# First FFN of a four-stage layer: two batches as dense expert pairs, two as tiles of chosen rows, with their QKV and key choice beside the attention

## The reference

```python
x = x + attn_a(layernorm(x))   # Haar wavelet mixing: q and v, transform over tokens, product, inverse, W_out
x = x + ffn(layernorm(x))      # 8 experts 128 -> 256 -> 128, relu squared; top 2 of softmax(x Wg), weights renormalised
x = x + attn_b(layernorm(x))   # 16 heads of 8; three softmaxes: band |i-j|<=128, top 128 keys of each head by score, first 64 keys
x = x + ffn(layernorm(x))
```

## Time and profile before

| what | us |
|---|---|
| median of 3 runs | 567.24 (566.62 to 568.09) |
| profiled execution | 567.43 |
| span of its instructions | 565.6 |
| PE busy | 517.7 (92%) |
| DVE busy | 405.7 (72%) |
| ACT busy | 349.4 (62%) |
| POOL busy | 271.4 (48%) |

### The profile page before, as it was taken

How to read it: one execution, slowest core, us unless ns; L and a number is a source line. 1 busy time by engine, 2 the same in 40 slices (tenths; PEclk the granted TensorE clock), 3 DMA queues, 4 the chain that set the end, 5 groups by cost and what they waited for, 6 DMA issues and landing times.

```text
span 565.6 us, 13219 instructions
## 1 busy us (share of the span) xinstructions
PE 517.7 (92%) x4483; PEld 320.4 (57%) x4483; DVE 405.7 (72%) x1426; ACT 349.4 (62%) x775; POOL 271.4 (48%) x429
## 2 busy tenths in 40 slices
PE   5899999999996889988998899999998999889996
PEld 2477776767672545444544454555545553567875
DVE  2547575698999799999967878788788795135335
ACT  6476666666640266666775577666775667667753
POOL 2402030160605994675408985859917246264540
PEclk9999999999996899999999999999999999999999
DMA  7970000000000000000000000001100011574606
GB/s 230 348 263 2 1 1 1 0 2 1 11 2 13 2 16 13 9 9 16 12 14 5 15 12 9 9 20 30 34 9 9 18 41 43 200 264 164 207 21 187
DMA packets 33443, 31.99 MB, mean 57 GB/s; under 512 B 7250, under 2 KB 28502, under 8 KB 33376
## 3 DMA queue, kind: packets, MB, share of 16 engines
q1 hardware_dynamic: 31616, 27.80, 15.9%
q0 software_dynamic: 1760, 3.35, 1.7%
HBM read 8.57 MB, written 12.00 MB: 36 GB/s over the span
## 4 chain that ended last, share of the span: by engine, by line
PE 62%; DVE 23%; issue 7%; POOL 3%; ACT 3%; DMA 1%; SPq 0%; DVEq 0%; POOLq 0%; ACTq 0%
PE BANK L1568 6%; PE BANK L1550 6%; PE BANK L1673 5%; PE BANK L1618 5%; PE BANK L1648 4%; PE BANK L1676 3%; DVE SW L1178 3%; PE BANK L1679 2%; PE BANK L1504 2%; PE BANK L1514 2%; DVE X L1160 2%; DVE M L1176 2%; PE BANK L1643 2%; PE BANK L1623 2%; POOL OH L556 2%
## 5 line engine op out<-in xcount | busy, mean ns | idle before, releaser
L822 ACT ACTIVATE PT<-BANK 128x256 f32<-128x256 f32 (+2 forms) x352 | 158.5, 492 | 96.6 <-PE BANK L1648 75.5
L556 POOL TENSOR_SCALAR OH<-IOTA,POS 128x128 bf16<-128x128 bf16 x240 | 139.5, 601 | 1.4 <-DVE POS L1192 1.0
L1219 DVE CUSTOM_DVE_ANT_0 XN_a<-BANK,BANDQ 128x256 f32<-128x256 f32 (+1 forms) x128 | 62.3, 487 | 23.2 <-PE BANK L1618 19.6
L1568 PEld LDWEIGHTS BANK<-W,PT 128*128 128x128 f32 x512 | 62.0, 192 | 15.2 <-issue 14.3
L1219 DVE CUSTOM_DVE_ANT_0 XN_c<-BANK,BANDQ 128x384 f32<-128x384 f32 (+1 forms) x128 | 62.3, 487 | 10.7 <-PE BANK L1618 9.6
L1568 PE MATMUL BANK<-W,PT 128*128 128x128 f32 x512 | 62.5, 275 | 0.0
L1550 PE MATMUL BANK<-XNT_ALL,W 128*128 128x512 f32 x128 | 60.6, 597 | 0.0
L733 ACT ACTIVATE PT<-BANK 128x512 f32<-128x512 f32 x64 | 38.0, 597 | 31.5 <-PE BANK L1550 31.0
L563 POOL TENSOR_TENSOR SUM<-NRM 128x128 f32<-128x128 f32 x16 | 7.3, 455 | 102.7 <-DVE NRM L1240 102.7
L1673 PE MATMUL BANK<-PT,V 128*32 128x256 f32 (+1 forms) x512 | 47.7, 444 | 2.0 <-ACT OS L831 0.4
L1224 DVE TENSOR_REDUCE QST<-BANK 128x4 f16<-128x512 f32 x64 | 41.6, 688 | 7.6 <-PE BANK L1623 7.5
(11 more groups left out here) (312 smaller groups left out, 1201.8 us busy)
## 6 DMA issues: line engine op xcount, KB each, us to landing
xs<-W SPq DMA_DIRECT2D x1, 6984.0 KB, 25.1
KZB<-W SPq DMA_DIRECT2D x16, 256.0 KB, 2.4
KZC<-W SPq DMA_DIRECT2D x15, 256.0 KB, 2.6
...
```

Source lines behind the costliest of these rows:

```text
L556: last = nc.gpsimd.tensor_scalar(OH[g % 2][:, i, t, :], IOTA[:, :], POS[:, t, c:c + 1], None, ALU.is_equal)
L822: nc.scalar.activation(PT[u % PT_RING][:, 0:w], P2_BANK[u % SCORE_RING][:, 0:w], ACT.Exp, scale=SCALE).then_inc(S["exp_done"], 1)
L1219: nc.vector.tensor_tensor_reduce(out=JUNK[v % 2][:, 0:n], in0=P1_BANK[v % SCORE_RING][:, 0:n], in1=BANDQ[:, off:off + n], scale=1.0, scala ...
L1568: last = mm(DOWN_BANK[n % 2][:, t * P:(t + 1) * P], HID_T[n % 2][hh][:, t * P:(t + 1) * P], W2[:, e, hh, :], start=(hh == 0), stop=(hh == ...
```

## The change

1. **Head.** Batches 0 and 1 run as two interleaved chains with buffers and banks of their own (CHAIN, CHAIN_BANK). ACT scales q by band while it copies it, and DVE multiplies it with v straight from PSUM. x of batch 1 is loaded second. `keep_busy` shrinks from 46 to 17 matmuls and uses zeros of W12. `with_bias` for batches 0 and 1 waits until both are normalized. The a steps of batches 2 and 3 go beside the pairs, 3 pairs apart.
2. **First FFN.** Only batches 0 and 1 are dense: 16 pairs. Batches 2 and 3 are routed as in the second FFN (class `Wave`, EARLY beside LATE): route at pairs 7 and 10, 16 scatters on POOL, table at pairs 11 and 12, then 23 tiles with their own row buffer and two result banks (`D_BANK["early"]`) instead of one. SP fills two DRAM areas with zeros instead of one. The results are loaded in four transfers, and POOL (not DVE) adds them to X.
3. **QKV of batches 0 and 1.** Batch 0 beside pairs 8 to 14. Batch 1 beside tiles 2 to 5.
4. **Key choice of batches 0 and 1.** Scores at tile 3, one or two half rounds a tile from tile 4, the last four behind the tiles, then mask, marks, places and the one-hots of group 0 between the first maxima. The spread of group 0's keys is issued at tile 11, and the gather of group 1 moves into group 0 at unit 2.
5. **Batches 2 and 3.** Statistics, normalization, transposes, scores and QKV move into groups 0 to 4 (C_AT, STATS_C, NORMS_C), through MISC. Their rounds move from groups 0 to 4 to groups 1 to 4.
6. **Batch 1's stacks and values** are split between ACT and POOL in groups 0 and 1, as those of batches 2 and 3 were already.

The core of the diff:

```diff
-SCORES_AT = (2, 3)
...
-MORE_ROUNDS = {(g, u) for g in range(5) for u in range(1, 22, 3)} - {(4, 13), (4, 16), (4, 19)}
-A_PERIOD = 5
...
+MORE_ROUNDS = {(g, u) for g in range(1, 5) for u in (1, 4, 6, 9, 12, 15, 17, 20)}
+A_PERIOD = 3
...
+EARLY = Wave("early", 2, 2)
+LATE = Wave("late", 0, 3)
+PAIRS = EARLY.first * E
...
+ROUNDS_TILE = {i: 1 + i % 2 for i in range(4, NT_EARLY)}
...
+C_AT = {(0, 11): ("turn", 2), (0, 16): ("turn", 3), (0, 18): ("score",),
+        (1, 7): ("qkv", 2, 0), (1, 11): ("qkv", 2, 1), (1, 16): ("qkv", 2, 2), (1, 18): ("qkv", 2, 3), (2, 7): ("qkv", 2, 4),
+        (2, 16): ("qkv", 3, 0), (3, 7): ("qkv", 3, 1), (3, 16): ("qkv", 3, 2), (4, 7): ("qkv", 3, 3), (4, 11): ("qkv", 3, 4)}
+STATS_C, NORMS_C = {(0, 1): 2, (0, 5): 3}, {(0, 8): 2, (0, 10): 3}
...
             stacks(0)
             rstd("c", 1)
+            for n in range(NT_EARLY):
+                tile_out(EARLY, n)
+                if n in VALUES_TILE:
+                    value_part(0, VALUES_TILE[n])
+            for slot in range(Y_RING):
+                pool.wait_ge(Y_OUT["early"][slot], 16 * slot_count(EARLY, slot))
+            global_values(0)
+            add_experts(2)
+            add_experts(3)
             pool.wait_ge(S["sel_done"], 1)
             onehot(1)
+            onehot(2, range(0, 2))
+            rstd("c", 2)
+            rstd("c", 3)
+            onehot(2, range(2, HG))
```

More of the change, by code:

```diff
@@ new lines, in results @@
+            def results(w):
+                for slot in range(Y_RING):
+                    sp.wait_ge(Y_OUT[w.tag][slot], 16 * slot_count(w, slot))
+                for b in range(w.count):
+                    for k in range(2):
+                        first = k * w.jt * P + b * L
+                        sp.dma_start(YB[w.tag][b][k], YT[w.tag][first:first + L, :].rearrange("(t p) d -> p t d", p=P)
+                                     ).then_inc(Y_IN[w.tag][b], 16)
+            sp.wait_ge(R["early"]["table"], 1)
@@ L546, in values, with onehot @@
                 pool.wait_ge(S["stack_v"], b + 1)
-            def onehot(g):
-                if g >= 2:
+            def onehot(g, parts=range(HG)):
+                if g >= 2 and 0 in parts:
                     pool.wait_ge(S["misc_full"], full("kv", g - 2))
-                for i in range(HG):
+                for i in parts:
                     c = g // GROUPS * SLOT + g % GROUPS * HG + i
@@ L1305, in _ @@
[L1305 to L1319 removed]
+            normalize("a", 1)
@@ new lines, in _ @@
+            dve.wait_ge(s["acc"], PAIRS)
+            stats("c", 1)
+            normalize("c", 1)
+            for i in range(NT_EARLY):
+                tile_y(EARLY, i)
+                if i in (SCORES_TILE, SCORES_TILE + 1):
+                    for t in range(2 * (i - SCORES_TILE), 2 * (i - SCORES_TILE) + 2):
+                        c_add(1, t)
+                if i == SCORES_TILE + 2:
+                    c_add(1, T)
+                rounds(0, ROUNDS_TILE.get(i, 0))
+            rounds(0, 2 * ROUNDS - taken[0])
@@ new lines, in _ @@
+            mask(0)
+            maxima(range(0, 3))
+            dve.wait_ge(S["sel_t"], 1)
+            marks(BANK[0]).then_inc(S["sel_t_s"], 1)
+            maxima(range(3, 7))
+            dve.wait_ge(S["sel_pos"], 1)
+            places(0, PLACE_BANK).then_inc(S["sel_done"], 1)
+            dve.wait_ge(S["sel_done"], 1)
+            for i in range(HG):
+                for t in range(T):
+                    last = nc.vector.tensor_scalar(OH[0][:, i, t, :], IOTA[:, :], POS[:, t, i:i + 1], None, ALU.is_equal)
@@ L1320, in _ @@
+            last.then_inc(S["onehot_dve"], 1)
+            maxima(range(7, 10))
+            gathered_kv(0)
+            maxima(range(10, UNITS_Q))
             maxima(range(UNITS_Q, UNITS_Q + FIRST_LEAD))
-            gathered_kv(1)
             for g in range(NG):
@@ L1498, in tile_up, with tile_turn @@
-            def tile_up(n):
-                pe.wait_ge(S["tile_xt"], n + 1)
+                if b == w.first + w.count - 1:
+                    for j in range(w.jt):
+                        last = mm(bank[:, T * E:T * E + E], TRI[:, 1, :], MSK[:, j, :], start=(j == 0), stop=(j == w.jt - 1))
+                return last
+            def tile_turn(w, n):
+                r = R[w.tag]
+                pe.wait_ge(TILE_IN[w.tag][n % IN_RING], 32 * (n // IN_RING + 1))
+                if n:
+                    pe.wait_ge(r["tile_xt"], n)
+                nc.tensor.transpose(T_BANK[w.tag][:, 0:P], XT_IN[w.tag][n % IN_RING][:, 0:D], IDENT[:, :]).then_inc(r["tile_t"], 1)
```

1313 lines of the change are left out of this document (734 added, 579 removed).

## The result

| | before | changed | forecast |
|---|---|---|---|
| median, us | 566.93 (566.61 to 568.09) | 558.72 (557.64 to 559.78) | 545 (531 to 558) |
| ratio to before, 95% interval | | 0.9851 (0.9827 to 0.9876) | 0.961 |
| span of the profiled execution | 565.6 | 556.8 | 543.0 |

The account below looks back on a forecast made before the run. PE was taken to bound the dense pairs, with PE and DVE both about 91% busy in groups 0 to 4. Terms -3.1 - 71.0 + 43 - 2.5 + 11 = -22.6 took 567.43 to 544.8, forecast 545 us, range 531 to 558.

Parts of the forecast that it names:

- Head and pairs: Start and first FFN: interleaved chains bring the first up to 23.15 us (-3.1); 16 dense pairs instead of 32 give -71.0.
- Tiles: New stage of 23 routed tiles after the pairs: +43 us, 1.6 a tile, bounds 36 to 53.
- Tile 4 waits until the last square, but SP issues one tile in 1.3 us: Tile stage: loads of tiles 0 to 3 come in time and later ones, at 1.3 us each, are covered.
- DVE has the longest queue and I take +43: Tile stage: DVE's work sums to 43 us, against POOL's 34 and PE's 31, and sets its length.
- Rival 1: Tile stage: bound by the ring of waits, not its longest queue; 10 us more, 555 in total; chance 0.14.
- Gap: Between the last tile and first attention unit: 21.3 us against 23.8 before, so -2.5.
- I add 1.0: Gap: POOL's four two-input additions beside DVE's 16 one-hots slow DVE by 1.0 us, giving 21.3 from 20.3.
- Groups 0 to 4: First five attention groups: moved work of batches 2 and 3 lengthens them from 92.0 to 103 us, +11, bounds 3 to 19.
- If DVE could be filled to 95% the five groups would take 100: Groups 0 to 4: added work of 10.9 us on DVE and 8.5 on PE partly fills idle time, giving 100 us.
- The POOL waits: Groups 0 to 4: POOL's later one-hots delay the gathers of groups 1 and 2, taking 100 us to 103.
- Rival 2: Groups 0 to 4: the work of batches 2 and 3 only moves there, growth 19.4 us, 553 in total; chance 0.12.
- Rival 4: Tile stage: PE's clock falls to 1.2 GHz, stage 67.5 us instead of 43, 569.5 in total; chance 0.04.

Follow-up runs that it names:

- e1: Changed kernel with the spread of group 0's keys issued before tile 16 instead of tile 11; ratio 0.9773 to the kernel before.
- e5: Changed kernel with all 32 half rounds of the key choice of batches 0 and 1 behind the 23 tiles; 574.6 us, ratio 1.0110 to before.
- e15: Changed kernel with keys spread at tile 16, POOL's group 1 one-hots before expert sums, QKV parts apart, batch 0's value parts ahead of the tiles; ratio 0.9715 to before.
- e12: Changed kernel with the half rounds behind the tiles and batch 0's value parts ahead of the first result; 572.4 us, ratio 1.0082 to before.
- e3: Changed kernel with POOL making group 1's one-hots before the expert sums; 556.0 us, ratio 0.9786 to before.
- e16: Changed kernel with keys at tile 16, POOL's one-hots before sums, QKV parts apart, and zero matmuls in PE's pauses into group 0; ratio 0.9716 on a slower chip.
- e4: Changed kernel with batch 2's QKV parts spread over groups 1 to 3 and batch 3's moved to groups 5 to 7; ratio 0.9805 to before.
- e2: Changed kernel with POOL waiting for DVE's 16 one-hots of group 0 before the expert sums; 558.1 us, ratio 0.9814 to before.
- e6: Changed kernel with 24 matmuls on zeros in PE's two pauses between the tiles and group 0; ratio 0.9828 to before.
- e14: Changed kernel with keys at tile 16, POOL's one-hots before sums, QKV parts apart, and 20 zero matmuls in PE's pauses before group 0; ratio 0.9695 to before.

## Why the prediction was wrong

**Head and pairs.** Right to 0.3 us: the first up matmul at 23.08 (forecast 23.15), the last down matmul ends at 97.2 (97.55), PE busy 99% in between. The pairs took 74.1 us in every run on the usual chips. Work removed from the engine that bounds a stage was the safest term, as forecast. That the head came out within 0.1 us is in part luck: in 5 of 18 runs of the same head the first up came 1.3 to 1.8 us later.

**Tiles, +4.7.** The step that failed first is the cover of the loads, "Tile 4 waits until the last square, but SP issues one tile in 1.3 us". That is true of the loads, but the spread of group 0's keys, listed in the change as issued at tile 11, stands between them and waits 6.6 us for ScalarE. The forecast had it at nothing, and it cost about 3 us (e1). The second is the way to the first result: 6.9 us from the last down matmul, not 5.5 (5.8 to 7.0 in the runs with the value parts in their place on the usual chips).

The step "DVE has the longest queue and I take +43" was wrong in its reason more than in its size. The forecast set 43 us of DVE against 34 of POOL, but the 43 have the 5.5 us before the first result in them and the 34 have not: on one footing it is 43 against 39.5. Measured, both queues need about 1.5 us a tile in the second half. Taking 28 half rounds off DVE left the stage as it was (e5), taking the value parts away from POOL's results did too (e15), and only both together gave 2 us (e12). With the wait of SP away and both queues in place the stage took 44.0 to 45.9 us, so the sum of 43 was near; no run takes the rounds out with that wait away. Rival 1, the ring of waits as the bound, was near in size (+10 forecast, +4.7 measured), and a wait was part of it, though in a queue that it does not name.

**Gap, +3.6.** The step that failed reads "I add 1.0" for DVE's one-hots beside POOL's additions. It was 4.3. The row behind it, 1.95 against 1.1 us for four normalizations beside one addition, holds the right price: one instruction held until the addition ended. But the price is due once for each addition, about 1.1 us a time, and there are four. The rest of the stage was right: with the contention away it took 20.9 us from the end of the last result (e3), with 20.3 forecast without it. The rule of the Trainium skill (GPSIMD Engine Reference, section 1, Specifications), by which the forecast had worked out 2 to 4 us more and had set them aside, gives the better sum here, since 3.3 us more were measured. The rule goes by the kind of the DVE instruction, and the traces agree in kind: the additions hold the one-hots and not the maxima. Which mode the one-hots ran in, no trace shows. The rule does not say which POOL instructions hold them, and there the runs differ (four additions 4.3 us, POOL's one-hots 0.2).

**Groups 0 to 4, +5.9.** The step that failed reads "If DVE could be filled to 95% the five groups would take 100". PE's added work was 11.7 us (95.4 against 83.7), where the forecast had 8.5; 0.9 of it is the low clock in group 0, which cost no time (e16). The idle time did not take in a part of the work but grew: PE's from 8.3 to 13.5 us, 9% to 12% of the stage. DVE ended at 86%. Crowding the QKV parts was 1.9 us (e4); what made the rest of the idle time is not shown. The POOL waits that the forecast priced at 3 us did not come: the one wait of PE for POOL's one-hots there is 0.3 us. They came when POOL was made to start later (e2, 2.9 us). Rival 2, growth by 19.4, was nearer to the truth (16.9) than the forecast was.

**Rival 4, the clock.** In the tiles the granted clock was 0.93 on the mean, so the rival did not come. From 147 to 171 us it was 0.50, in a place that the forecast had not asked about, and there it cost next to nothing (e16), because DVE, not PE, is the bound. A swing as the Trainium skill describes it (TensorE: Matmul & The Clock Gate, section "HAM oscillation") is to be seen in e6 and e14, where the clock rose and fell within 15 us around a pause of PE, with no price in this stage.

**Range.** Tiles and groups came out inside their own bounds (tiles 36 to 53, groups +3 to +19); the gap had none of its own in the range, though the forecast names 2 to 4 us for it by the rule. The range let the bounds cancel, and all three stages missed on the same side: two because they were built on full engines and covered loads, the third by the contention. With the upper bounds of tiles and groups added as they stand it would have reached 563, with head and pairs 566.
